# A vision tower in one kernel: shorter passages into the spectral mixing, and the next groups' normalisation roots at the end of a window's slots

## The reference

```python
for i in range(LAYERS):                      # 4
    x1 = spectral_conv(h, w1, w2)            # rfft2, 12 x 12 complex modes mixed over channels, irfft2
    x2 = einsum('bchw,oc->bohw', h, conv_w[i]) + conv_b[i]
    h = layer_norm(x1 + x2, ln_g[i], ln_b[i])
    if i < LAYERS - 1: h = gelu(h)
h = gelu(h @ fc1_w + fc1_b); h = gelu(h @ fc2_w + fc2_b); h = h @ fc3_w + fc3_b
```

```python
h = h + scan(layernorm(h))        # ... y + x * D_skip + xf * D_skip, xf = x flipped in time; then @ W_out.T
u = rmsnorm(layernorm(h), ln1_w)  # q, k with rotary turns, causal softmax, 4 heads
x = layernorm(h) + attention(u) @ wo.T
f = rmsnorm(x, ln2_w)             # top 2 of 8 experts: silu(f @ w1.T) * (f @ w3.T) @ w2.T
```

## Time and profile before

| | us |
|---|---|
| median of 3 runs (lowest, highest) | 7341.99 (7340.01, 7343.35) |
| the profiled execution's own time | 7339.24 |
| its span | 7337.5 |

### The profile page before, as it was taken

How to read it: one execution, slowest core, us unless ns; L and a number is a source line. 1 busy time by engine, 2 the same in 40 slices (tenths; PEclk the granted TensorE clock), 3 DMA queues, 4 the chain that set the end, 5 groups by cost and what they waited for, 6 DMA issues and landing times. The chain is left out here.

```text
span 7337.5 us, 138677 instructions
## 1 busy us (share of the span) xinstructions
PE 6634.3 (90%) x43890; PEld 4056.0 (55%) x43890; DVE 4609.9 (63%) x7185; ACT 4417.8 (60%) x8385; POOL 3735.1 (51%) x1348
## 2 busy tenths in 40 slices
PE   8999799999799998899998899999999578888888
PEld 3444566666566665666665544444444255555555
DVE  8999477777477776577776333333333477777774
ACT  5666466766466766466765577777777434444443
POOL 8999278777178776277775244444444100000000
PEclk9999899999899999999999999999999788888888
DMA  2333455554455554555554311111111333333330
GB/s 98 112 110 113 168 164 165 166 170 158 167 169 165 167 169 150 175 169 165 166 170 146 126 47 53 48 47 47 54 47 47 104 81 74 74 74 74 74 74 3
DMA packets 597030, 835.12 MB, mean 114 GB/s; under 512 B 451944, under 2 KB 493032, under 8 KB 531304
## 3 DMA queue, kind: packets, MB, share of 16 engines
q1 hardware_dynamic: 596968, 834.34, 36.6%
HBM read 477.60 MB, written 356.58 MB: 114 GB/s over the span
## 5 line engine op out<-in xcount | busy, mean ns | idle before, releaser
L949 POOL TENSOR_TENSOR sb_rstd<-sb_var,sb_minus_half 128x16 f32<-128x16 f32 x1280 | 3689.7, 2899 | 2047.8 <-DVE sb_var L900 1019.6
L691 DVE TENSOR_TENSOR sb_unit<-H,sb_rstd 128x512 f32<-128x512 f32 x768 | 529.1, 689 | 684.0 <-POOL sb_rstd L949 545.9
L508 PE MATMUL H<-sb_conv_block,sb_act_in 128*128 128x128 f32 x6144 | 825.3, 283 | 35.4 <-DMA sb_act_in<-act_scratch 28.7
L508 PEld LDWEIGHTS H<-sb_conv_block,sb_act_in 128*128 128x128 f32 x6144 | 731.6, 192 | 150.1 <-issue 140.9
L613 ACT ACTIVATE sb_act_px<-sb_unit 128x512 f32<-128x512 f32 x768 | 484.0, 630 | 499.5 <-DVE sb_unit L697 499.5
L2295 POOL TENSOR_TENSOR blk_pos<-blk_pos,blk_mag 128x260 f32<-128x260 f32 x32 | 22.8, 734 | 1337.3 <-ACT blk_mag L1961 1337.3
L636 ACT ACTIVATE sb_act_out<-TC 128x512 f32<-128x512 f32 x768 | 447.7, 583 | 180.8 <-PE TC L523 180.8
L912 DVE COPY sb_act_out<-TC 128x512 f32<-128x512 f32 x256 | 177.0, 691 | 595.3 <-PE TC L758 595.3
L775 PE MATMUL M<-sb_dense,sb_fc_w 128*64 128x512 f32 x2048 | 521.7, 609 | 30.4 <-ACT sb_dense L858 25.4
L697 DVE TENSOR_TENSOR sb_unit<-sb_unit,sb_shift_row 128x512 f32<-128x512 f32 x768 | 531.4, 692 | 26.1
L694 DVE TENSOR_TENSOR sb_unit<-sb_unit,sb_gain_row 128x512 f32<-128x512 f32 x768 | 531.2, 692 | 26.2
(11 more groups left out here) (274 smaller groups left out, 12749.6 us busy)
## 6 DMA issues: line engine op xcount, KB each, us to landing
act_scratch<-sb_act_out SPq DMA_DIRECT2D x256, 1024.0 KB, 3.9
sb_act_in<-act_scratch SPq DMA_DIRECT2D x256, 1024.0 KB, 5.3
spectrum_in<-sb_f_sb SPq DMA_DIRECT2D x512, 78.0 KB, 1.8
sb_x_in<-spectrum_in SPq DMA_DIRECT2D x48, 832.0 KB, 4.4
spectrum_out<-sb_y_sb SPq DMA_DIRECT2D x48, 832.0 KB, 4.6
sb_z_in<-spectrum_out SPq DMA_DIRECT2D x512, 78.0 KB, 5.1
blk_rows_b<-scan_rows SPq DMA_DIRECT2D x128, 260.0 KB, 6.6
blk_rows_bb<-scan_rows SPq DMA_DIRECT2D x128, 260.0 KB, 7.5
```

Source lines behind the costliest of these rows:

```text
L508: e.matmul(H[j][:, 128 * u:128 * u + 128], act_in[p][:, 128 * b:128 * b + 128], conv_block[:, :], start=(u == 0), stop=False, skip_group_c ...
L691: e.tensor_tensor(rows, H[k][:, :].rearrange("p (y c) -> p y c", c=C), rstd[k][:, :].unsqueeze(2).to_broadcast([128, 16, C]), ALU.mult).th ...
L949: e.tensor_tensor(rstd[j][:, :], var[j][:, :], minus_half[:, :], ALU.pow).then_inc(rstd_ready, 1)
```

## The change

In the tokenizer: the columns of gain and shift are loaded once at the start, for the last layer only (`param_in` 21 instead of 13). `sp_layer` is split into `sp_rows` (two rows) and `sp_conv` (conv weights, bias and the first two mixing weights), which is issued during the pass before. `conv_in` is a new semaphore. At the end of a pass SP waits for the stored spectrum and issues the first two `x_in` ahead of the rows; then it loads the first two `act_in` of the next pass ahead of the mixing's loop. The conv's product uses H0, and the first combine uses H0 to H3, with copies from there; PE does both ahead of its waits for ACT, and the first `turn` waits for the four copies. DVE centres ky 0 right behind `dve_layer`.

In the block: the scan's and the experts' guesses and roots move from the head to the end of the window before (`guesses` on ACT in slot 24, `roots` on DVE behind slot 26). `MEAN_AT` 23 to 22, `H1_AT` 25 to 24. The experts' square stays in slot 23, now ahead of the table load. The keys' products go to banks 1 and 2, and wait for ACT's reading of these instead of for the queries' `rope`; w3 of slots 0 and 1 waits for the keys' `rope`. The first gate cast moves into slot 0, behind `res` and w1. The skip product moves from slot 9 to 12 and takes the sum `xs = xn + xf`, which POOL makes, so one product less.

```diff
@@ tokenizer, SP
+        def sp_load_act(e, P, p, n):
             at_least(e, h_ready, 8 * P + 4 * p - 4)
             e.dma_start(act_in[p][:, :], act_d[n]).then_inc(ld[p], 16)
+        def sp_load_spectrum(e, p, n):
...
+        def sp_rows(e, norm):
+            g, b = norm
             e.dma_start(gain_row[:, :], g.partition_broadcast(128)).then_inc(layer_in, 16)
             e.dma_start(shift_row[:, :], b.partition_broadcast(128)).then_inc(layer_in, 16)
+        def sp_conv(e, layer):
+            e.dma_start(conv_raw[:, :], io["conv_w"][layer]).then_inc(conv_in, 16)
+            e.dma_start(bias_raw[:, :], io["conv_b"][layer].unsqueeze(1)).then_inc(conv_in, 16)
+            for p in range(2):
+                e.dma_start(w_raw[p][:, :], io["w_mix"][layer, p]).then_inc(w_in[p], 16)
...
             def layer_body(layer, last):
                 for p in range(2):
-                    e.dma_start(w_raw[p][:, :], io["w_mix"][layer, p]).then_inc(w_in[p], 16)
+                    e.wait_ge(st_x[p], 32 * halves * (layer + 1))
+                for p in range(2):
+                    sp_mix_load(e, 0, p, layer)
                 e.wait_ge(act_ready, 8 * halves * (layer + 1))
-                sp_layer(e, layer + 1, layer, (io["ln_g"][layer], io["ln_b"][layer]))
+                sp_rows(e, (io["ln_g"][layer], io["ln_b"][layer]))
+                for p in range(2):
+                    e.wait_ge(st_a[p], 16 * halves * (layer + 1))
+                    sp_load_act(e, halves * (layer + 1), p, p)
                 mix(layer)
...
-                        sp_load(e, base, p, p, False)
+                        sp_load_spectrum(e, p, p)
+                    if not last:
+                        sp_conv(e, layer + 1)
@@ tokenizer, PE
+            banks = H if isinstance(m, int) and q == 0 else COMBINED
...
+            if zero:
+                e.wait_ge(w_mix_s, 4 * q0 + 4)
             turn(0)
...
                 e.wait_ge(unit_ready, 8 * halves * (layer + 1))
+                pe_layer(e, layer)
+                pe_combine(e, 0, 0, layer)
                 e.wait_ge(act_ready, 8 * halves * (layer + 1))
                 e.wait_ge(f2_ready, 2 * halves * (layer + 1))
-                pe_layer(e, layer)
...
-                pe_combine(e, 0, 0, layer)
@@ block
-        WO_AT, X2_AT, H1_AT = 22, 23, 25
+        WO_AT, X2_AT, H1_AT = 22, 23, 24
-        SKIP_AT = 9
+        SKIP_AT = 12
-        MEAN_AT, VARIANCE_AT = 23, 24
+        MEAN_AT, VARIANCE_AT = 22, 24
...
+                    if n == 0:
+                        gate_cast(g, 0)
                     if k == 0:
                         wait(e, "ug", g, x + 1)
+                    if n < 2 and attn is not None:
+                        wait(e, "rope", attn, 5 + n)
...
-                    e.matmul(B[7][:, 0:TOK], wskip[:, :], xn[:, :], start=True, stop=False, skip_group_check=True)
-                    e.matmul(B[7][:, 0:TOK], wskip[:, :], xf[:, :], start=False, stop=False, skip_group_check=True)
+                    wait(e, "both", g)
+                    e.matmul(B[7][:, 0:TOK], wskip[:, :], xs[:, :], start=True, stop=False, skip_group_check=True)
...
-                    wait(e, "rope", ga, 2)
-                    e.matmul(B[5][:, 0:TOK], wt("wk_t"), un[:, :], start=True, stop=True)
-                    e.matmul(B[6][:, 0:TOK], wk_rot[:, :], un[:, :], start=True, stop=True).then_inc(sig["qk"], 1)
+                    if scan:
+                        wait(e, "bc", gs)
+                        wait(e, "soft_pos", gs)
+                    e.matmul(B[1][:, 0:TOK], wt("wk_t"), un[:, :], start=True, stop=True)
+                    e.matmul(B[2][:, 0:TOK], wk_rot[:, :], un[:, :], start=True, stop=True).then_inc(sig["qk"], 1)
...
-                    gate_cast(gx, 0)
@@ block, ACT
-                        if n == PARTS * NE - 1:
-                            e.preload_act_table_set("natural_log_exp_and_others")
...
+                    if n == X2_AT:
                         moe_square(w + 1, moe1)
+                        if moe:
+                            e.preload_act_table_set("natural_log_exp_and_others")
...
+                    if n == VARIANCE_AT:
+                        guesses(w + 1, scan1, moe1)
                 attention_square(w + 1, attn1)
@@ block, DVE (the head's scan and expert steps are now roots(w, scan, moe), called in before too)
+                roots(w + 1, scan1, moe1)
@@ block, POOL
+                    e.tensor_tensor(xs[:, :], xn[:, :], xf[:, :], ALU.add).then_inc(sig["both"], 1)
```

More of the change, by code:

```diff
@@ L1055, in dve_mix @@
                 e.tensor_copy(w_mix[p][:, :].rearrange("r (k b c g a) -> r k b g c a", k=NK, b=2, c=4, g=8)[:, :, b, :, :, a],
[L1056 to L1063, removed]
-            g, b = norm
[L1065 to L1073, removed]
+                              banks[s][:, 0:NK * C].rearrange("r (k g c) -> r k g c", g=8, c=4)).then_inc(w_mix_s, 1)
+        def sp_rows(e, norm):
+            g, b = norm
             e.dma_start(gain_row[:, :], g.partition_broadcast(128)).then_inc(layer_in, 16)
             e.dma_start(shift_row[:, :], b.partition_broadcast(128)).then_inc(layer_in, 16)
+        def sp_conv(e, layer):
[3 more added lines that the diff above has]
+                e.dma_start(w_raw[p][:, :], io["w_mix"][layer, p]).then_inc(w_in[p], 16)
         def dve_layer(e, n):
-            e.wait_ge(layer_in, 160 + 192 * (n + 1))
+            e.wait_ge(conv_in, 32 * (n + 1))
             e.tensor_copy(conv_rep[:, :].rearrange("o (g c) -> o g c", g=4),
@@ L1142, in _, with one_pass @@
             e.dma_start(fc3_bias[:, :], io["fc3_b"].partition_broadcast(128)).then_inc(param_in, 16)
-            sp_layer(e, 0, None, (io["ln0_g"], io["ln0_b"]))
-            def one_pass(first, last, start):
+            for u in range(4):
+                e.dma_start(gain[32 * u:32 * u + 32, :], io["ln_g"][LAYERS - 1].unsqueeze(1)).then_inc(param_in, 16)
+                e.dma_start(shift[32 * u:32 * u + 32, :], io["ln_b"][LAYERS - 1].unsqueeze(1)).then_inc(param_in, 16)
+            sp_rows(e, (io["ln0_g"], io["ln0_b"]))
+            sp_conv(e, 0)
+            def one_pass(first, last, start, layer=None):
                 base = start
@@ L1938, in window, with before @@
                     guess(moe_n, "x")
+            def before(w, scan, attn, moe):
+                scan_square(w, scan)
+                guesses(w, scan, moe)
+            def window(w, scan, attn, moe, scan1, attn1, moe1):
+                gs, ga, gx = w + 1, w, w - 1
+                old = moe and not (isinstance(gx, int) and gx == 0)
                 if attn:
@@ L2215, in gate_steps, with roots @@
                 return shifted, probabilities, first, second
-            def window(w, scan, attn, moe, scan1, attn1, moe1):
-                gs, ga, gx = w + 1, w, w - 1
-                shifted, probabilities, first, second = gate_steps(gx)
+            def roots(w, scan, moe):
+                gs, gx = w + 1, w - 1
                 if scan:
@@ L2247, in window, with before @@
                     e.tensor_copy(by_token(xf[:, :]), by_token(xn[:, :])[:, :, ::-1]).then_inc(sig["flipped"], 1)
+            def before(w, scan, attn, moe):
+                roots(w, scan, moe)
+            def window(w, scan, attn, moe, scan1, attn1, moe1):
+                gs, ga, gx = w + 1, w, w - 1
+                shifted, probabilities, first, second = gate_steps(gx)
                 if attn:
@@ L2283, in window @@
                         expert_slot(gx, n)
-            windows(e.Fori, lambda *at: None, window)
+                roots(w + 1, scan1, moe1)
+            windows(e.Fori, before, window)
         @block.gpsimd
```

58 lines of the change are left out of this document (28 added, 30 removed).

## The result

The changed kernel takes 7289.79 us (median of 4, 7283.87 to 7294.44), the kernel before 7341.0: a ratio of 0.993, 95% interval 0.9914 to 0.9945. It is faster by 51 us, where 119 were forecast, and outside the stated range of 7172 to 7262. The profiled execution has a span of 7287.6 us. The head's last product now starts at 5718.14 instead of 5756.66, so the tokenizer gave 38.5 us (forecast 39.8). From the block's first product to the end of the span it was 7337.5 - 5766.70 = 1570.8 us and is 7287.6 - 5728.10 = 1559.5: 11.3 us, where 79 were forecast. Nearly the whole miss lies in the block.

A forecast was written before the change was run, and what follows sets the result against it. PE, 90% busy, waits in a window's head; DVE paces slots 4 to about 13, then PE. Tokenizer 39.8 plus block 79 gives 118.8 us off 7339.24, so 7220.4; plus 2.75 gives 7223 us, range 7172 to 7262 (8 in 10).

The forecast's parts named there:

- The passages: Tokenizer, between passes and mixing: loads made a pass earlier shorten waits; 39.8 us in all, between 25 and 48.
- the last layer: Tokenizer's last passage into the mixing: DVE also waits for the fold's product, so the gain is 6.8 us, bounds 4 and 10.
- The late weights of ky 2: Mixing, first three layers: weights queued behind other loads land near 16 us after the pass, costing 1.8 us each, bounds 0 and 3.
- The way out: From mixing into the next pass: pixels' conv before the wait, `z_in` issued earlier; 7.3 us over four layers, bounds 3 and 11.
- The start: Tokenizer's start: four more DMAs and 416 KB of weights ahead of the first images; loss of 2.5 us, between 1.9 and 3.0.
- The roots: Block's head: roots moved to the window before start the projections 3.3 us earlier per window, bounds 2.0 and 3.8.
- The gate cast in slot 0: Block, slot 0: `res` and w1 run while PE idled before the cast; 1.0 us per window, bounds 0 and 1.9.
- the case that the prediction had as its lower bound: Gate cast in slot 0: gain 0 if ACT's copy comes so early that the cast waits for PE.
- The clock: Block's projections: PE's idleness is split, so it may keep 2.4 GHz; 1.0 us per window, between 0 and 1.7.
- The rival of the smaller gain: Block: clock falls at the projections as before, slot 0 gives nothing, 3.3 us per window: 7251 us; chance 0.18.
- The skip product: Block, move from slot 9 to 12: gain 0, as PE's idleness behind the exponentials covers it; without cover, cost 0.9.
- The rival that named a low clock as the way to lose: Block: PE idles behind the keys until gates are turned, and the slots run at 1.2 GHz: 7363 us, slower; chance 0.03.

The follow-up runs named there:

- the clock held: Useless products in PE's idle head stretches: kernel before 7303.7 us; changed kernel 7222.35 us, or 7219.03 with the skip product in slot 9.
- the roots alone: Changed tokenizer, and in the block only the roots, moved means and `h1` copy; keys, gate cast and skip product as before: 7259.78 us.
- five useless ones more: Changed kernel with useless products in three idle stretches: 3 ahead of the projections, 14 behind the keys, 5 ahead of the skip product in slot 12: 7304.41 us.
- the block alone: Changed block with the tokenizer of the kernel before: 7326.66 us, 12.9 us less than the kernel before.

## Why the prediction was wrong, point by point

**The passages** were right in their mechanism, and their sum, 38.5 against 39.8, is nearer than its terms: that part is luck. First products at 9.6, 10.5 and 9.3 us behind the pass, where 10.4 was worked out. From the pass to the end of the mixing it took 6.4, 9.3 and 10.4 us less (forecast 9.4 each), and 5.8 in the last layer (6.8). The late weights of ky 2 were there at 17.0 us (forecast 16) and held up ky 1. The way out gained 3.6, 3.9, 3.1 and 1.8 us, 12.4 in all against 7.3: the pixels' conv was done in the wait, and the spectrum was there 3.9 us after its issue (894.70 to 898.62), where 5.3 had been taken as a bound. 4.8 of it went again, as the three middle passes took 1.1 to 2.2 us more each than before, which nothing in the forecast had. The start cost 2.0 (2.5), and the last pass gave 1.0.

**The roots** were right: 3.25 us a window in the head against 3.3, unfilled and with the clock held. The 41.8 us of the roots alone, against 49, also hold the 1.9 that the clock gave in the head and the 1.8 that it took in slots 1 and 2.

**The gate cast in slot 0** was wrong: 1.0 a window forecast, and with the keys less than 1 us in the whole kernel where the skip product is in slot 9. From the gates to the first silu the cast's place changes nothing (5.44 and 5.43 us): in the window shown above ACT's copy is there 1.21 us behind the gates, and the cast then waits for PE's `res` and w1 until 2.37. It is the case that the prediction had as its lower bound. With the keys and the gate cast the head is 0.18 us shorter (24.15 to 23.97), and slots 1 and 2 take 0.16 more.

**The clock** is the first step that failed. Forecast was a gain of 1.0, from projections at full clock. With the roots alone they had it (1.4 us up to the gates), but slots 1 and 2 took 1.8 back. In the changed kernel most windows had little or nothing of it: from the projections to the gates they take 13.09 us in the mean, against 13.24 before, so 0.15 came in place of 1.0, and slots 1 and 2 took 2.17 back. I had set a price on the low stretch that I saw at the projections, and none on the one behind the keys, which reached to the first slots. It doesn't follow the head: with the skip product in slot 9 it ends 28.7 us behind the last silu, 29.4 before, while the head got 5.4 us shorter. What had been hidden under waits comes to lie on work. The rival of the smaller gain, with 3.3 a window, was right about these parts; its 7251 is near the 7259 of the kernel without the skip product's move, but it held that the rest would be nothing, not that it would be lost.

**The skip product** is the second and larger step: "0", against 26 to 31 us in the changed kernel. The cover was real, PE did idle for 3.47 us. What failed was the step that idle time of PE is free to fill. With the roots it wasn't; in the kernel before, and with the head's clock held, it was for this product, though five useless ones more cost 82 us. The rival that named a low clock as the way to lose had the mechanism, but put it behind the keys, where undoing it changed nothing.

Added up in this order: 41.8 for the roots, 0.6 for keys and gate, -30.6 for the skip product are 11.8, where 79 were forecast; the block alone measured 12.9. In the other order the skip product takes 13.6 and keys and gate 16.4. The sum holds, and the shares belong to the order: the edits don't add, as the prediction's terms do.

**What stays open.** That the product's move costs its time by the clock is shown in part: with the head's clock held it costs 3 us, not 31, and work put into the same stretch costs 69 by a wait that moved to slot 14. How the row of equal windows breaks can be read from the granted clock. With the roots alone the low stretch behind the exponentials starts 52.45 us behind the silu of the last slot 23 in the third full window and a little earlier in each that follows, 52.30 in the ninth, and lasts 6.8 us. In the tenth it starts at 52.28 and lasts 10.2: slots 14 to 16 take 9.68 us instead of 8.51, and in the next head the clock falls at the projections too (25.53 instead of 24.15). With the skip product moved as well, the starts are 52.33, 52.30 and 52.28, then comes the same break with four more unequal windows, and then the three starts again. So the equal windows of the roots alone lie close to a point at which the row breaks. What sets that point, and why the moved product brings the loop back to it again and again, isn't shown; I have no run that sets it alone.

## What to carry to other kernels

Where PE's clock falls behind a wait, give every wait of PE a second price: the products that then run slow, and whether PE or another engine sets the pace where they stand. A wait that lies ahead of another engine's stretch is the right place for it, and filling it can push the wait into PE's own; filling the one ahead of PE's own work paid here, even with useless products. Before an edit of a part of a per cent is judged, look whether all windows of a loop still have one period. If they don't, compare it with the clock held and window by window, or its sign can be that of the pattern and not of the edit.

## What the runs showed of the hardware

- The best kernel of the study does more work than the changed one: 17 useless products a window in the head, and the skip product in slot 9: 7219.03 us, 1.65% below the kernel before and 71 us below the changed kernel.
- Six useless products a window, in 3.5 us of PE's idle time, for which nothing waits, made a kernel slower by 69 us, 0.95% (7259.15 to 7328.39).
- Edits that are worth nothing with the skip product in slot 9 (7259.8, 7259.2, 7263.4) gave 7273, 7277, 7290 and 7292 with it in slot 12. There all periods but two were 88.2 to 88.9 us, and here they were a mixture, mostly of 87.0 to 93.2.
- Over the whole profiled execution the mean granted clock was 0.953 before and 0.953 after: the average shows nothing of this. Only stages do.
